# A fused attention and feed-forward kernel: the feed-forward part's preparation moved into attention's program, in smaller pieces, with the first normalisation on ScalarE

## The chip, the cores and the metric

The kernel runs on one core of a Trainium2 chip. The metric is device time of one execution in microseconds (us). TensorE (PE) multiplies matrices, VectorE (DVE), ScalarE (ACT) and GpSimd (POOL) work elementwise, SyncE (SP) issues most transfers. Each engine runs its own list of instructions in order, and waits on semaphores where it needs another's result.

## The reference

The input x has 2048 tokens of 256 values in fp32. Two layers follow each other, each wrapped as x + layernorm(f(layernorm(x))):

```python
# attention: 16 query heads and 8 key heads of 128, in pairs; causal
p = softmax(q1 k1 / sqrt(128)) - lam * softmax(q2 k2 / sqrt(128))   # two maps a head pair
o = p @ v                      # v is 256 wide
o = o * rsqrt(mean(o*o) + eps) * subln_w * (1 - LAMBDA_INIT)
out = o @ out_w.T + out_b
# feed-forward: fwht is the normalised Walsh-Hadamard transform
h = fwht(x * SU_ug) / 64
h = silu(h @ W_gate.T * (Ws_gate * 64)) * (h @ W_up.T * (Ws_up * 64))    # 1024 wide
out = (fwht(h * SU_dp) / 64) @ W_down.T * (Ws_dp * 64)
```

fwht is linear, so the kernel folds it, the signs and the scales into the weights.

## The kernel before

Every fp32 matrix product is done as three matmuls in a faster format (fp32r), since each operand is split into a high part (a copy, by ScalarE) and a low part (the difference, by VectorE or GpSimd): high x high, high x low, low x high. So each thing that TensorE reads has first passed over two other engines.

**Attention.** There are 4 groups of two query-head pairs that share keys and values. A group has 16 duos; a duo is one tile of 128 query tokens for each of its two head pairs, cut into 5 chunks of up to 512 keys (17 blocks of 128 together). Each duo has two halves, one for each softmax map (m = 0, 1). `attention_steps` writes the order of the whole of attention as one list of steps: S (scores of a chunk), T (transposes of mixed probabilities), PV (products with v), OT and OP (transpose and projection of an output), QP, K, V (projections), X (transposes of normalised x), LN and NX (statistics and normalising of x), WQ, WK, WO (splits of weights). A string for each half (`HALVES`, `HEAD`, `TURN_OF_GROUP`, `LAST_HALVES`) gives the order of its steps by letters. The engines walk through the same list, ScalarE and VectorE with lags of a step for some kinds (`SCALAR_LAGS`, `VECTOR_LAGS`). ScalarE computes exponentials (L543) and high parts (L558), VectorE row maxima (L647, L652) and low parts (L662), GpSimd mixes the two maps (L802, L805). `PAIR_ORDER` orders the tiles within a group; each output tile is added to `acc` in every group, so after the last group's visit it is final.

**Between.** A second block of the program folds weights. ScalarE and GpSimd scale raw weights (L1072, L1119), TensorE transposes them (L980, L989), both parts are split (L1028, L1045), TensorE multiplies by the Hadamard matrix of 128 (L1011, L1020), whose result is scaled and split (L1034, L1052). w_down first goes through three butterfly stages on VectorE and GpSimd (L1109, L1110). VectorE normalises the first 512 tokens in `norms` in four parts, each for 4 tiles.

**Feed-forward.** A third block runs over 4 chunks of 512 consecutive tokens. For each of 8 slices of 128 of the 1024 inner values TensorE computes gate and up (6 matmuls of 512 columns each, L1241), ScalarE Silu (L1280) and the high part of h (L1285), VectorE the product (L1330), GpSimd the low part (L1388). Then the product with folded w_down (L1256, L1258), whose rows are normalised and stored. Normalising of the next chunk is done between, in four parts of 4 tiles.

## Time and profile before

| | us |
|---|---|
| median of 3 runs | 1442.15 |
| lowest run | 1440.96 |
| profiled execution, its own time | 1443.69 |
| its span | 1441.6 |
| TensorE busy in the span | 1374.2 (95%) |
| VectorE busy | 1045.2 (73%) |
| ScalarE busy | 875.5 (61%) |
| GpSimd busy | 866.3 (60%) |

The span goes from the first to the last instruction; the execution's own time holds some 2 us around it. Busy shares are means over three unlike stages (attention, folding, feed-forward), so each stage has to be read by itself. Matmuls overlap in the records: how long TensorE takes for one is told by the distance between two starts, not by the duration of one.

### The profile page before, as it was taken

The page shows a single profiled execution, that of the slowest core. Times are in us where ns is not written, and L with a number is a line of the kernel's source. Part 1 is how long each engine was busy: PE and PEld are TensorE (multiplying, and loading weights), DVE is VectorE, ACT ScalarE, POOL GpSimd, SP SyncE. Part 2 cuts the span into 40 slices and gives each one's busy share as a digit, 9 for nine tenths or more (in the row PEclk, how much of TensorE's full clock was granted, in tenths as well). Part 3 has the DMA queues.
Part 4 walks back from the last instruction along what each step waited for, and adds up shares of the span by engine and source line. Part 5 has one row for each costly group of instructions (what it writes and reads, how often), then busy time and mean ns, then how long its engine had stood idle before and what let it go on. Part 6 is the DMA issues. An engine that isn't in the chain of part 4 may idle for free. (4 is left out here: it accounts for less than half of the span.)

```text
span 1441.6 us, 26446 instructions
## 1 busy us (share of the span) xinstructions
PE 1374.2 (95%) x8344; PEld 1214.6 (84%) x8344; DVE 1045.2 (73%) x2628; ACT 875.5 (61%) x2465; POOL 866.3 (60%) x1332
## 2 busy tenths in 40 slices
PE   5899999999999999999999999999999999569998
PEld 4789999988989999889899998898999998547887
DVE  5677778776687788766777777777778877576654
ACT  3466666666576766666666676656766667353331
POOL 7556666665666666647676656556766666335454
PEclk9999999999999999999999999999999999879999
DMA  3000000000000000000000000000000000310000
GB/s 128 1 30 1 1 1 1 1 16 1 10 22 2 1 2 1 16 1 1 31 1 1 2 1 2 16 1 1 1 1 1 1 1 1 104 43 1 11 16 33
DMA packets 14806, 18.36 MB, mean 13 GB/s; under 512 B 4432, under 2 KB 12752, under 8 KB 14288
## 3 DMA queue, kind: packets, MB, share of 16 engines
q1 hardware_dynamic: 13712, 15.35, 3.3%
q8 instruction: 71, 1.16, 0.3%
q10 hardware_dynamic: 960, 1.32, 0.3%
q14 instruction: 63, 0.52, 0.1%
HBM read 14.58 MB, written 2.10 MB: 12 GB/s over the span
## 5 line engine op out<-in xcount | busy, mean ns | idle before, releaser
L543 ACT ACTIVATE e<-score_bank,negmx 128x512 f32<-128x512 f32 (+2 forms) x640 | 394.4, 626 | 72.8 <-DVE negmx L656 71.8
L805 POOL TENSOR_TENSOR e<-e,e 128x512 f32<-128x512 f32 (+3 forms) x256 | 294.5, 1150 | 21.4
L652 DVE TENSOR_REDUCE mx<-score_bank 128x1 f32<-128x512 f32 (+1 forms) x384 | 244.6, 638 | 27.2 <-PE score_bank L448 25.8
L446 PE MATMUL score_bank<-k_hi,q_hi 128*128 128x512 f32 (+2 forms) x640 | 253.9, 397 | 8.2 <-ACT e L543 6.1
L788 POOL TENSOR_TENSOR inv_s<-s,neg_one 128x1 f32<-128x1 f32 x128 | 71.0, 555 | 314.1 <-DVE s L772 313.6
L468 PE MATMUL turn_bank<-v_hl,pT_hi 128*128 128x512 f32 x679 | 251.5, 404 | 3.8 <-DVE pT_lo L662 3.8
L448 PE MATMUL score_bank<-k_hi,q_lo 128*128 128x512 f32 (+2 forms) x640 | 231.9, 362 | 0.0
L447 PE MATMUL score_bank<-k_lo,q_hi 128*128 128x512 f32 (+2 forms) x640 | 231.3, 361 | 0.0
L470 PE MATMUL turn_bank<-v_hl,pT_lo 128*128 128x256 f32 x679 | 190.8, 281 | 0.0
L802 POOL TENSOR_SCALAR e<-e,ratio 128x512 f32<-128x512 f32 (+3 forms) x256 | 177.4, 693 | 12.4
L647 DVE CUSTOM_DVE_ANT_0 score_bank<-score_bank,mask 128x384 f32<-128x384 f32 (+3 forms) x256 | 143.3, 560 | 52.2 <-PE score_bank L448 50.8
L468 PEld LDWEIGHTS turn_bank<-v_hl,pT_hi 128*128 128x128 f32 x679 | 128.1, 189 | 30.4 <-issue 4.7
L446 PEld LDWEIGHTS score_bank<-k_hi,q_hi 128*128 128x128 f32 x640 | 121.0, 189 | 26.5 <-ACT e L543 9.3
L448 PEld LDWEIGHTS score_bank<-k_hi,q_lo 128*128 128x128 f32 x640 | 120.5, 188 | 14.1
L543 ACT ACTIVATION_READ_ACCUMULATOR e<-score_bank,negmx 128x1 f32 x640 | 131.5, 205 | 0.0
L470 PEld LDWEIGHTS turn_bank<-v_hl,pT_lo 128*128 128x128 f32 x679 | 128.8, 190 | 0.5
L447 PEld LDWEIGHTS score_bank<-k_lo,q_hi 128*128 128x128 f32 x640 | 121.8, 190 | 4.8
L468 PE MATMUL sum_bank<-v_hl,pT_hi 128*128 128x512 f32 x281 | 103.4, 401 | 1.3 <-DVE pT_lo L662 1.3
L558 ACT ACTIVATE pT_hi<-turn_bank 128x384 fp32r<-128x384 f32 (+3 forms) x140 | 75.5, 540 | 46.7 <-PE turn_bank L455 46.0
L662 DVE TENSOR_TENSOR pT_lo<-turn_bank,pT_hi 128x384 fp32r<-128x384 f32 (+3 forms) x140 | 84.3, 602 | 3.9 <-ACT pT_hi L558 3.4
L1388 POOL TENSOR_TENSOR h_lo<-h_f,h_hi 128x512 fp32r<-128x512 f32 x32 | 41.5, 1295 | 68.9 <-ACT h_hi L1285 68.9
L818 POOL TENSOR_TENSOR rms<-rms_b,half_neg 128x1 f32<-128x1 f32 x128 | 73.5, 574 | 10.7
(266 smaller groups left out, 3548.9 us busy)
## 6 DMA issues: line engine op xcount, KB each, us to landing
w_raw<-in_w_qkv_dram SPq DMA_DIRECT2D x3, 1024.0 KB, 4.8
w_raw<-in_w_o_dram SPq DMA_DIRECT2D x4, 512.0 KB, 3.3
out_dram<-d_out SPq DMA_DIRECT2D x16, 128.0 KB, 1.7
x_in<-in_hidden_dram SPq DMA_DIRECT2D x3, 512.0 KB, 9.5
x_res<-in_hidden_dram SPq DMA_DIRECT2D x1, 1536.0 KB, 13.0
w_raw<-in_w_qkv_dram ACTq DMA_DIRECT2D x2, 512.0 KB, 8.2
raw<-in_w_up_dram SPq DMA_DIRECT2D x2, 512.0 KB, 5.5
raw<-in_w_gate_dram SPq DMA_DIRECT2D x2, 512.0 KB, 7.7
```

Source lines behind the costliest of these rows:

```text
L446: pe.matmul(bank[:, 0:w], qh, kh, start=True, stop=False)
L447: pe.matmul(bank[:, 0:w], qh, kl, start=False, stop=False)
L448: pe.matmul(bank[:, 0:w], ql, kh, start=False, stop=True).then_inc(s_full, 1)
L468: pe.matmul(bank[:, :], pT_hi[:, q % PT_SLOTS, b * P:(b + 1) * P], v_hl[:, kt, :], start=(kt == 0), stop=False)
L470: mm = pe.matmul(bank[:, 0:HID], pT_lo[:, q % PT_SLOTS, b * P:(b + 1) * P], v_hl[:, kt, 0:HID], start=False, stop=(kt == i))
L543: act.activation(e, S[k % NS][:, 0:w], ACT.Exp, bias=negmx[:, d % 2, m, s:s + 1], accum_out=ssum[:, d % 4, s, m, c:c + 1]).then_inc(s_act, 1)
L558: act.activation(pT_hi[:, q % PT_SLOTS, 0:w], bank_for(kind, what)[:, 0:w], ACT.Copy).then_inc(t_hi, 1)
L647: dve.tensor_tensor_reduce(out=S[k % NS][:, 0:w], in0=S[k % NS][:, 0:w], in1=mask[:, BANK - w:], scale=1.0, scalar=LOWEST, op0=ALU.add, op ...
L652: dve.tensor_reduce(mx[:, d % 2, m, s, c:c + 1], S[k % NS][:, 0:w], X, ALU.max)\
L662: dve.tensor_tensor(pT_lo[:, q % PT_SLOTS, 0:w], bank_for(kind, what)[:, 0:w], pT_hi[:, q % PT_SLOTS, 0:w].bitcast(F32), ALU.subtract)\
L802: pool.tensor_scalar(b, b, ratio[:, d % 4, s:s + 1], 0.0, ALU.mult, ALU.add)\
L805: pool.tensor_tensor(a, a, b, ALU.add).then_inc(p_pool, 1)
```

## The change

The two later blocks of the program are gone. Their work becomes steps of the same list: HAD (the Hadamard matrix, built on GpSimd), FB (sum or difference of two halves of gate and up weights, which arrive already transposed), FH (split of that), F (fold by the matrix and split), N (one part of normalising for two tiles: parts 0 to 3 as before, each in two halves), Z (transposes of normalised tiles), G and U (gate and up of one slice, with HH for h's split), DB (pieces of w_down's butterflies), DN (product with w_down). The last group visits its tiles in another order (`LAST_ORDER`), outermost pairs first, so that a feed-forward chunk's four tiles (`chunk_tiles`) are final before attention ends. Strings for single halves of the last group (`LAST_GROUP`) say where N and Z (letter N), FH and F (f), FB (b), HAD (H) stand; in `LAST_HALVES` each U issues one gate or up block, and `with_gated` hangs further steps behind them. Tiles of attention whose last use has passed hold the new data. Scales of gate and up are applied at Silu and at the product rather than to the weights.

At the start, normalising of x (NX) goes from GpSimd to ScalarE, transfers are reordered, four of eight V units of the first group come before its first scores, and the split of w_o comes a half later.

```diff
+WS_COL = SUBLN_COL + CT
+SU_COL = WS_COL + 2 * JT
+SUD_COL = SU_COL + CT
+COLS = SUD_COL + JT
...
 PAIR_ORDER = (3, 7, 4, 2, 5, 1, 6, 0)
+LAST_ORDER = (0, 7, 1, 6, 2, 5, 3, 4)
...
-HEAD = {0: 'SKSVSVQSVS', 1: 'SVSVSQVSS', 2: 'SVSSQSVS', 3: 'TSTSSOSTPSoQTPPTP'}
+HEAD = {0: 'SKSVSQSVS', 1: 'SVSSQSVS', 2: 'SSSQSS', 3: 'TSTSSOSTPSoQTPPTP'}
...
-LAST_HALVES = ('ToTPTToOP', 'TTOTPPTPO', 'ToTTTOoPo')
+LAST_GROUP = {5: 'TSTSSOSTPSoQTPPTPH', 12: 'TSSTSSTPbTSoQTPPbPTO',
+              13: 'TSTSSNOSTPSoNQTPPTP', 14: 'TSSTSSTPNTSoQTPPNPTO', 15: 'TSTSSNOSTPSfoNQTPPTP',
+              16: 'TSSTSSTPNTSfoQTPPNPTO', 17: 'TSTSSNOSTPSfoQNTPPTP', 18: 'TSSTSSTPbTSfoQTPPbPTO',
+              20: 'TSSTSSTPTSfoQTPPPTO', 21: 'TSTSSNOSTPSfoNQTPPTP', 22: 'TSSTSSTPNTSfoQTPPNPTO',
+              23: 'TSTSSNOSTPSfoNQTPPTP', 24: 'TSSTSSTPNbTSoQTPPNbPTO', 25: 'TSTSSNOSTPSoQNTPPTP',
+              26: 'TSSTSSTPTSfoQTPPPTO', 27: 'TSTSSOSTPSfoQTPPTP', 28: 'TSSTSSfTPbTSfoQTPPbPTO',
+              30: 'TSSTSSfTPTSfoQTPPPTO', 31: 'TSTSSfOSTPSfoQTPPTP'}
+LAST_HALVES = ('ToTPTToOPUU', 'UTUTOTPUPTPO', 'TUoTUTTOUoPUo')
...
+def chunk_tiles(c):
+    return (2 * c, 2 * c + 1, TILES - 2 - 2 * c, TILES - 1 - 2 * c)
+def pair_of(u):
+    return (LAST_ORDER if u // (DUOS // 2) == GROUPS - 1 else PAIR_ORDER)[u % (DUOS // 2)]
...
-    for kind, what in (("LN", 0), ("WK", 0), ("NX", 0), ("LN", 1), ("WQ", 0), ("X", 0), ("X", 1), ("NX", 1),
-                       ("K", (0, 0, 0)), ("LN", 2), ("X", 2), ("X", 3), ("K", (0, 1, 0)), ("NX", 2), ("QP", (0, 1, 0)),
-                       ("K", (0, 0, 1)), ("QP", (0, 1, 1)), ("LN", 3), ("X", 4), ("X", 5), ("K", (0, 1, 1)), ("NX", 3),
-                       ("QP", (0, 0, 0)), ("K", (0, 0, 2)), ("LAM", None), ("QP", (0, 0, 1)), ("X", 6), ("X", 7),
-                       ("K", (0, 1, 2)), ("K", (0, 0, 3))):
+    for kind, what in (("LN", 0), ("LN", 1), ("NX", 0), ("WK", 0), ("NX", 1), ("X", 0), ("X", 1), ("WQ", 0), ("LN", 2),
+                       ("X", 2), ("X", 3), ("NX", 2), ("K", (0, 0, 0)), ("K", (0, 1, 0)), ("X", 4), ("X", 5), ("LN", 3),
+                       ("V", (0, 0)), ("V", (0, 1)), ("QP", (0, 1, 0)), ("QP", (0, 1, 1)), ("K", (0, 0, 1)), ("NX", 3),
+                       ("K", (0, 1, 1)), ("V", (0, 2)), ("V", (0, 3)), ("LAM", None), ("QP", (0, 0, 0)),
+                       ("QP", (0, 0, 1)), ("K", (0, 0, 2)), ("X", 6), ("X", 7), ("K", (0, 1, 2)), ("K", (0, 0, 3))):
...
+    norms = [x for c in range(2) for x in norm_steps(c, range(4)) + turn_steps(c)]
+    folds = [x for n in range(0, 8, 2) for x in fold_steps(n)]
+    hadamard = [("HAD", None)]
+    added_up = [("FB", n) for n in range(8)]
+    gated = [0]
+    with_gated = {
+        2: norm_steps(2, (0,)), 4: norm_steps(2, (1,)) + [("DB", 0), ("DB", 1)], 5: [("DB", 2), ("DB", 3)],
+        6: norm_steps(2, (2,)) + [("DB", 4), ("DB", 5)], 7: [("DB", 6), ("DB", 7)], 8: norm_steps(2, (3,)),
+        9: [("DB", i) for i in range(8, 12)], 10: [("DB", i) for i in range(12, 16)], 11: [("FH", 8), ("FH", 9)],
+        12: [("F", 8), ("F", 9), ("FH", 10), ("FH", 11)], 13: [("F", 10), ("F", 11)], 14: turn_steps(2),
+        16: norm_steps(3, (0,)), 18: norm_steps(3, (1,)), 20: norm_steps(3, (2,)), 22: norm_steps(3, (3,))}
+    def emit_gated():
+        k, up = divmod(gated[0], 2)
+        gated[0] += 1
+        emit("U" if up else "G", k)
+        if not up and k > 0:
+            emit("HH", k - 1)
+        if up:
+            for what in with_gated.get(k, ()):
+                emit(*what)
...
-    while exps_due or factors_due or mixes_due:
-        emit("END", None)
-    for what in to_turn:
-        emit("OT", what)
-    for what in to_project:
-        emit("OP", what)
+    assert not (exps_due or factors_due or mixes_due or norms or folds or added_up)
+    while to_turn or to_project:
+        if to_turn:
+            emit("OT", to_turn.pop(0))
+        emit_gated()
+        if to_project:
+            emit("OP", to_project.pop(0))
+    for c in range(FFN_CHUNKS):
+        while gated[0] < 2 * JT * (c + 1):
+            emit_gated()
+        if c + 1 == FFN_CHUNKS:
+            emit("HH", JT * FFN_CHUNKS - 1)
+        if c > 0:
+            for n in range(QB * (c - 1), QB * c):
+                emit("DN", n)
+                if n == QB:
+                    for what in turn_steps(3):
+                        emit(*what)
+    for n in range(QB * (FFN_CHUNKS - 1), QB * FFN_CHUNKS):
+        emit("DN", n)
+    emit("DEND", None)
...
+            def wug(f, co):
+                return ((k_hi[:, co, 3 * BANK:], k_lo[:, co, 3 * BANK:]),
+                        (v_hl[:, 12 + co, :], v_hl[:, 14 + co, :]),
+                        (wq_hi[:, co, :], wq_lo[:, co, :]),
+                        (v_hl[:, 10 + co, :], w3_lo[:, co, :]))[f]
+            wd_hl = v_hl[:, 0:JT, :]
+            wd_a, wd_b = e1[:, 0:4, :], e1[:, 5:9, :]
+            wsd_row = out_b_row
+            z = bv
+            gate = w_raw[:, 1, :].rearrange("p (a n) -> p a n", a=2)
+            h_f = v_sum
...
+                sp.wait_ge(kv_dve, last_value_split + 1)
+                load_input(0)
+                sp.wait_ge(t_full, t_use["Z", (0, 1)] + 1)
+                load_input(1)
+                sp.wait_ge(folded_ready, 2)
+                sp.dma_start(raw_w(2), w_ug[2]).then_inc(raw_landed[2], 16)
+                sp.wait_ge(folded_ready, 4)
+                sp.dma_start(raw_w(3), w_ug[3]).then_inc(raw_landed[3], 16)
+                sp.wait_ge(t_full, t_use["Z", (1, 1)] + 1)
+                load_input(2)
+                sp.wait_ge(t_full, last_turn[CHUNKS * (ALL_DUOS - 1) - 1] + 1)
+                sp.dma_start(wd_a, w_d.rearrange("p (q n) -> p q n", q=4)).then_inc(wd_landed, 16)
...
+                    elif kind in ("G", "U"):
+                        c, jt = divmod(what, JT)
+                        up = kind == "U"
+                        b = 2 * (what % 2) + up
+                        if what < 2:
+                            pe.wait_ge(s_act, last_score - (last_score - b) % NS + 1)
+                        else:
+                            pe.wait_ge(h_ready if up else g_act, what - 1)
+                        if jt == 0 and not up:
+                            pe.wait_ge(t_lo, t_use["Z", (c, 1)] + 1)
+                        if c == 0 and jt % 2 == 0 and not up:
+                            pe.wait_ge(t_lo, t_use["F", jt + 1] + 1)
+                        at, n = 2 * (jt % 2) * P + up * P, 0
+                        for ct in range(CT):
+                            w_hi_part, w_lo_part = wug(jt // 2, ct)
+                            for w, x in ((w_hi_part, xT_hi), (w_hi_part, xT_lo), (w_lo_part, xT_hi)):
+                                mm = pe.matmul(S[b][:, :], w[:, at:at + P], x[:, ct, Z_COLS[c]:Z_COLS[c] + BANK],
+                                               start=(n == 0), stop=(n == 5))
+                                n += 1
+                        mm.then_inc(u_full if up else g_full, 1)
...
+                    elif kind == "NX":
+                        act.wait_ge(rstd_ready, what + 1)
+                        for t in range(4 * what, 4 * what + 4):
+                            act.activation(x_in[:, t, :], x_in[:, t, :], ACT.Identity, bias=shift[:, t:t + 1],
+                                           scale=rstd[:, t:t + 1]).then_inc(xn_ready, 1)
...
+                    elif kind == "N":
+                        c, part, half = what
+                        base = 24 * c + 8 * part + 4 * half
+                        pair = [(x, chunk_tiles(c)[x]) for x in (2 * half, 2 * half + 1)]
+                        if part == 0:
+                            dve.wait_ge(r_free, max(r_use["OP", last_visit[t]] for _, t in pair) + 1)
+                        if part in (0, 2):
+                            dve.wait_ge(n_step, base)
+                            for x, t in pair:
+                                dve.bn_stats(n_stats[:, x, :], acc[:, t, :]).then_inc(n_step, 1)
+                            dve.wait_ge(n_step, base + 2)
+                            for x, t in pair:
+                                dve.bn_aggr(n_mv[:, x, :], n_stats[:, x, :]).then_inc(n_step, 1)
+                        elif part == 1:
+                            dve.wait_ge(y_rstd, c + 1)
+                            dve.wait_ge(xr_landed, 32 * c + 32)
+                            for x, t in pair:
+                                dve.scalar_tensor_tensor(out=acc[:, t, :], in0=acc[:, t, :], scalar=n_rs[:, x:x + 1],
+                                                         in1=z[:, x, :], op0=ALU.mult, op1=ALU.add)\
+                                   .then_inc(n_step, 1)
+                            dve.wait_ge(n_step, base + 2)
+                            for x, t in pair:
+                                dve.tensor_scalar(acc[:, t, :], acc[:, t, :], n_mr[:, x:x + 1], None, ALU.subtract)\
+                                   .then_inc(n_step, 1)
+                        else:
+                            dve.wait_ge(z_rstd, c + 1)
+                            for x, t in pair:
+                                dve.tensor_scalar(z[:, x, :], acc[:, t, :], n_mv[:, x, 0:1], n_rs[:, x:x + 1],
+                                                  ALU.subtract, ALU.mult).then_inc(z_ready, 1)
...
+                    elif kind == "U":
+                        b, at = 2 * (what % 2) + 1, WS_COL + 2 * (what % JT) + 1
+                        dve.wait_ge(g_act, what + 1)
+                        dve.wait_ge(u_full, what + 1)
+                        if what == 0:
+                            dve.wait_ge(wt_lo_ready, 8)
+                        if what >= 2:
+                            dve.wait_ge(h_lo_ready, what - 1)
+                        dve.scalar_tensor_tensor(out=h_f[:, what % 2, :], in0=S[b][:, :], scalar=col[:, at:at + 1],
+                                                 in1=gate[:, what % 2, :], op0=ALU.mult, op1=ALU.mult)\
+                           .then_inc(h_ready, 1)
...
+                    elif kind == "FB":
+                        f, co = divmod(what, CT)
+                        pool.wait_ge(raw_landed[f], 16)
+                        if what == 0:
+                            pool.wait_ge(had_ready, 1)
+                        if what >= 2:
+                            pool.wait_ge(wt_lo_ready, what - 1)
+                        pool.tensor_tensor(folded[:, co, :], raw_w(f)[:, 0, :], raw_w(f)[:, 1, :],
+                                           ALU.subtract if co else ALU.add).then_inc(folded_ready, 1)
...
+                    elif kind == "DB" and what < 8:
+                        if what < 4:
+                            pool.wait_ge(wd_landed, 16)
+                            pool.wait_ge(wsd_landed, 16)
+                            unit = wd_a[:, what, :].rearrange("p (a n) -> p a n", a=2)
+                            scales = wsd_row[:, :].rearrange("p (a n) -> p a n", a=1).broadcast_to([P, 2, HID])
+                            pool.tensor_tensor(unit, unit, scales, ALU.mult).then_inc(wd_pool, 1)
+                        else:
+                            pool.wait_ge(wd_pool, 2 if what < 6 else 4)
+                            pool.wait_ge(t_full, last_turn[CHUNKS * ALL_DUOS - 1] + 1)
+                            units, op = slice(what // 6 * 2, what // 6 * 2 + 2), what % 2
+                            pool.tensor_tensor(wd_b[:, units, op * HID:(op + 1) * HID], wd_a[:, units, 0:HID],
+                                               wd_a[:, units, HID:2 * HID], ALU.subtract if op else ALU.add)\
+                                .then_inc(wd_pool, 1)
...
-        with ExitStack() as ffn:
...
```

**VectorE, half 14 of the last group.** Before, around the mixing of that duo's fourth chunk (e is a chunk of exponentials, pT_lo the low part of transposed probabilities):

```order
L662 TENSOR_TENSOR pT_lo<-proj_bank,pT_hi 128x384
L780 SCALAR_TENSOR_TENSOR e_64<-e_65,ratio,e_64 128x512
L652 TENSOR_REDUCE mx<-score_bank 128x1
L662 TENSOR_TENSOR pT_lo<-sum_bank,pT_hi 128x384
L647 ISA score_bank,mx<-score_bank,mask 128x384
L647 ISA mx 128x1
L656 TENSOR_REDUCE negmx<-mx 128x1
```

And in the changed kernel:

```order
L1234 SCALAR_TENSOR_TENSOR e_64<-e_65,ratio,e_64 128x384
L1023 TENSOR_TENSOR pT_lo<-sum_bank,pT_hi 128x384
L1174 SCALAR_TENSOR_TENSOR acc<-acc,n_rs,bv 128x256 x2
L1179 TENSOR_SCALAR acc<-acc,n_mr 128x256 x2
L1008 ISA score_bank,mx<-score_bank,mask 128x384
L1008 ISA mx 128x1
L1017 TENSOR_REDUCE negmx<-mx 128x1
```

Between a split of probabilities and the masked maximum of the next scores now stand four instructions that normalise two tiles.

**TensorE, the end of attention.** Before, behind the last output projection:

```order
L512 MATMUL turn_bank<-wo_lo,oT_hi 128x256
L512 MATMUL turn_bank<-wo_hi,oT_lo 128x256
L245 UNCONDITIONAL_BRANCH
L969 UNCONDITIONAL_BRANCH
L980 MATMUL turn_bank<-ident,raw 128x128 x8
L980 MATMUL sum_bank<-ident,raw 128x128 x4
```

In the changed kernel, the first gate block (S banks from xT and folded weights, which lie in k_hi and k_lo):

```order
L689 MATMUL turn_bank<-v_hl,pT_lo 128x256
L782 MATMUL score_bank<-xT_hi,k_hi 128x512
L782 MATMUL score_bank<-xT_lo,k_hi 128x512
L782 MATMUL score_bank<-xT_hi,k_lo 128x512
```

The transposes of raw weights are gone, and gate and up stand between products of attention's last duo.

**ScalarE, the start.** Before:

```order
L617 ACTIVATE wkv_hi<-w_raw 128x1024
L610 ACTIVATE wq_hi<-w_raw 128x1024
L604 ACTIVATE xT_hi<-score_bank 128x512 x2
L593 ACTIVATE k_hi<-turn_bank,col 128x512
L604 ACTIVATE xT_hi<-score_bank 128x512 x2
```

Changed:

```order
L872 ACTIVATE x_in<-x_in,shift,rstd 128x256 x4
L890 ACTIVATE wkv_hi<-w_raw 128x1024
L872 ACTIVATE x_in<-x_in,shift,rstd 128x256 x4
L877 ACTIVATE xT_hi<-score_bank 128x512
L883 ACTIVATE wq_hi<-w_raw 128x1024
L877 ACTIVATE xT_hi<-score_bank 128x512 x2
```

The copy of the first transposes now follows two rounds of normalising.

## Rows read from the trace of the kernel before

**Rows 1.** The page: the granted clock in 40 slices, in tenths.

```profile
PEclk9999999999999999999999999999999999879999
```

**Rows 2.** Busy time by stretch; columns: us, then each engine's busy us (instructions), clock, DMA.

```profile
600.00:610.00 10.00, 9.04 (x53) 7.43 (x52) 8.87 (x23) 6.99 (x20) 5.08 (x11) 1.00 0.15 54
1108.00:1118.00 10.00, 10.00 (x66) 8.84 (x64) 9.15 (x22) 6.76 (x21) 4.96 (x7) 1.00 0.00 1
1005.00:1215.00 210.00, 209.95 (x1330) 189.20 (x1329) 163.19 (x417) 142.73 (x430) 137.79 (x222) 1.00 0.00 1
0.00:50.00 50.00, 31.44 (x161) 26.30 (x162) 27.52 (x73) 18.31 (x31) 28.11 (x35) 0.97 0.28 93
...
1250.00:1300.00 50.00, 30.87 (x117) 23.66 (x118) 36.59 (x80) 23.62 (x43) 14.16 (x16) 0.69 0.32 105
1300.00:1350.00 50.00, 48.25 (x221) 38.62 (x220) 30.95 (x74) 19.83 (x36) 26.74 (x29) 1.00 0.00 1
```

**Rows 3.** TensorE's timeline; columns: start, duration, line, operation, tiles, shapes, idle before and releaser.

```profile
17.89 0.63 PE L481 MATMUL turn_bank<-xT_hi,wkv_lo 128*128 128x512 f32 x1
18.32 0.63 PE L481 MATMUL turn_bank<-xT_hi,wkv_hi 128*128 128x512 f32 x1
...
904.43 0.47 PE L468 MATMUL turn_bank<-v_hl,pT_hi 128*128 128x512 f32 x1 [0.96 <-DVE pT_lo L662]
...
911.49 0.39 PE L446 MATMUL score_bank<-k_hi,q_hi 128*128 128x512 f32 x1
911.72 0.40 PE L447 MATMUL score_bank<-k_lo,q_hi 128*128 128x512 f32 x1
```

**Rows 4.** TensorE's timeline at the end of attention and of folding.

```profile
1225.67 0.50 PE L468 MATMUL turn_bank<-v_hl,pT_hi 128*128 128x512 f32 x1 [1.11 <-DVE pT_lo L662]
...
1244.66 0.36 PE L512 MATMUL turn_bank<-wo_hi,oT_hi 128*128 128x256 f32 x1 [1.00 <-DVE oT_lo L678]
...
1245.33 0.28 PE L512 MATMUL turn_bank<-wo_hi,oT_lo 128*128 128x256 f32 x1
...
1292.30 0.79 PE L1241 MATMUL score_bank<-xT_hi,wug_hi 128*128 128x512 f32 x1 [1.41 <-DVE xT_lo L1305]
```

**Rows 5.** The timeline of the start.

```profile
7.75 5.56 POOL L854 TENSOR_SCALAR x_in<-x_in,mv,rstd 128x256 f32<-128x256 f32 x4
...
13.46 1.94 PE L429 MATMUL score_bank<-ident,x_in 128*128 128x128 f32 x8 [13.46 <-POOL x_in L854]
...
16.90 0.77 PE L481 MATMUL turn_bank<-xT_hi,wkv_hi 128*128 128x512 f32 x1 [1.51 <-DVE xT_lo L727]
...
72.17 0.50 PE L446 MATMUL score_bank<-k_hi,q_hi 128*128 128x512 f32 x1 [3.89 <-ACT e L543]
...
73.53 0.69 PE L446 MATMUL score_bank<-k_hi,q_hi 128*128 128x384 f32 x1 [0.32 <-ACT e L543]
```

**Rows 6.** Groups by line and shape; columns: count, busy us, mean ns, idle before.

```profile
L1388 POOL TENSOR_TENSOR h_lo<-h_f,h_hi 128x512 fp32r<-128x512 f32 x32 | 41.5, 1295 | 68.9 <-ACT h_hi L1285 68.9
...
L1052 DVE SCALAR_TENSOR_TENSOR wug_lo<-score_bank,su_col,wug_hi 128x512 fp32r<-128x512 f32 x8 | 5.8, 746 | 1.7 <-ACT wug_hi L1034 1.7
...
L1072 ACT ACTIVATE raw<-raw,scaled_col 128x256 f32<-128x256 f32 x8 | 3.6, 499 | 11.8 <-DMA raw<-in_w_up_dram 11.8
```

**Rows 7.** DMA issues of the page; last columns: KB, us to landing.

```profile
raw_d<-in_w_down_dram SPq DMA_DIRECT2D x1, 1024.0 KB, 9.8
```

**Rows 8.** VectorE's timeline while it normalises four tiles.

```profile
1257.24 1.38 DVE L897 TENSOR_SCALAR acc<-acc,y_mr 128x256 f32<-128x256 f32 x4
...
1298.50 1.39 DVE L886 BATCH_NORM_STATS2 y_stats<-acc 128x6 f32<-128x256 f32 x4
1299.93 0.38 DVE L889 BATCH_NORM_AGGREGATE y_mv<-y_stats 128x2 f32<-128x6 f32 x4
1304.40 2.00 DVE L893 SCALAR_TENSOR_TENSOR acc<-acc,y_rs,x_res 128x256 f32<-128x256 f32 x4
1306.43 2.13 DVE L897 TENSOR_SCALAR acc<-acc,y_mr 128x256 f32<-128x256 f32 x4
```

889 lines of the change are left out of this document (363 added, 526 removed).

## The prediction

> **What bounds the kernel now.** I read the page first. TensorE's clock is at full speed in nearly every slice [rows 1], and in an ordinary stretch of 210 us of attention TensorE is busy for 209.95 us, VectorE for 163.2 (78%), ScalarE for 142.7, GpSimd for 137.8 [rows 2]. So attention is bound by TensorE, and only two things shorten the time: less work on TensorE, or fewer holes in it. The timeline says what full pace is: a matmul of 512 columns starts 0.23 us after the one before it, and at the lower of the clock's two levels (1.2 against 2.4 GHz) 0.43 us [rows 3].
>
> Then I looked for the holes. The large one lies between attention and the feed-forward part: the last output projection starts at 1245.33, the first gate matmul at 1292.30 [rows 4]. In the 50 us around it TensorE is busy for 30.9 at a granted clock of 0.69, while VectorE is busy for 36.6: folding weights and normalising is a chain over the other engines [rows 2]. Just ahead of it attention runs dry: five waits of 0.6 to 1.3 us from 1225.67 to 1244.66, 5.0 us together [rows 4]. The third place is the start: first transposes at 13.46, first projection at 16.90, and a wait of 3.89 us at 72 [rows 5]; TensorE is busy for 31.4 of the first 50 us [rows 2].
>
> **The large hole.** The change puts folding, the weights' splits, and the normalising of chunks 0 and 1 into halves 12 to 31 of the last head group; the first gate matmul then follows the last ordinary product steps on TensorE directly. What goes is 1292.30 less 1245.45 (the last projection's start plus 0.12), 46.9 us. What of it must still be done on TensorE moves: 24 fold matmuls at 0.23, 5.6 us (40 before; the transposes of raw weights are gone, and the gate/up fold's 128-step now adds or subtracts halves of the weights on GpSimd), and the 8 transposes of z for chunk 0, 0.9 us (eight took 1.94 at the lower level [rows 5]). Net **-40.4**. Nothing hides these 6.5 us: TensorE is the bound there.
>
> **The dry end of attention.** The last three halves now carry gate and up matmuls between transposes and products, 10 blocks of six (1.4 us each). Each of the five waits is shorter than one such block. But the table load for Silu (once, as before) and the gate's activation now stand ahead of probability copies on ScalarE. I take **-3.5** of the 5.0; ends 0 and -5. In the later feed-forward part the 50 us from 1300 have 1.75 us of idle TensorE [rows 2], spent on the next chunk's transposes that are now early: **-1.5**.
>
> **GpSimd while w_down is folded.** It had all of w_down's butterfly halves inside the hole. Now pairs 4 to 7 of gate and up give GpSimd, beside h_lo at 1.30 us [rows 6], two additions or products each of the same shape: 3.9 us against TensorE's 2.8 for twelve matmuls, 4.4 us too much over four pairs, with roughly one pair of slack since h_f waits for the h_lo of two pairs ago. Queued behind them on GpSimd is the next h_lo; VectorE's h_f waits for that, TensorE's next bank for h_f. **+2.5**; ends 0 and +9.8, the latter if w_down itself (1 MB, 9.8 us before [rows 7]) has not landed: its load waits on SyncE for the transposes of the last duo but one, some 15 us ahead of its first use.
>
> **VectorE in the last group: what I fear most.** Two halves issue 30 score matmuls, 17 transposes and 34 products, and 28 matmuls for output and queries: 109. The 210 us hold 1330 [rows 2], so two halves take 17.2 us, one half 8.6. Added to VectorE per chunk of four tiles: statistics twice (1.39 and 0.38 each time), scale and add 2.00, subtract 2.13, final scale 2.1: 9.8 us [rows 8]. Chunk 0's lie in halves 13 to 16 with two splits of folded weights (0.75 each, as the folded row [rows 6]), chunk 1's in 21 to 24 with three. Four halves on TensorE: 34.4 us, 35 with what is added. On VectorE: 0.78 x 34.4 = 26.7, plus 9.8 plus 1.5 (or 2.25): 38.0 and 38.7. VectorE becomes the bound of eight halves. If it could be busy all the time, that costs 3.0 + 3.7 = 6.7 us. The busiest stretch in which TensorE lost nothing has VectorE at 9.15 of 10 us; another at 8.87 lost 0.96 us of TensorE [rows 2]. At 92% it costs 6.3 + 7.1 = 13.4. I take **+10**, between them. The ends are +3 (the other engines run ahead and absorb it) and +34: all that is added, 2 x 9.8 + 16 x 0.75 + 4 transposed halves of z at 0.7, exposed. ScalarE gets 20 copies of 0.6 in 175 us and stays under 80%; GpSimd gets eight additions of 1.3 and four sets of 1.3: under 80% too. Both I cost at nothing beyond this.
>
> Here the durations themselves depend on the neighbour: the same four subtractions took 1.38 us at 1257 in the hole, and 2.13 at 1306 beside GpSimd's h_lo [rows 8]. I used the slow values, since GpSimd is busy for 66% of attention [rows 2]. GPSIMD Engine Reference of the Trainium skill (Specifications) says why that may be: GpSimd shares its SBUF interfaces with VectorE, with contention when VectorE runs in a two-port mode or reads two SBUF inputs. The splits of folded weights now read two SBUF tiles, where they read a PSUM bank; by that rule they would cost more than 0.75, and GpSimd's mixing would slow down too. That speaks against the change; no row of this case prices it for the split.
>
> **The start.** Normalising moves from GpSimd (5.56 us for four tiles [rows 5]) to ScalarE, at about 0.5 a tile (scaling raw weights of the same shape took 0.50 [rows 6]), 2 us for four; statistics of tiles 4 to 7 come before weights. x is thus ready at about 10 instead of 13.3. But on ScalarE the copy of the first transposes now stands behind the second normalisation and a weight copy of 1.1, so the first projection starts near 16.5, hardly earlier than 16.90. The gain comes after: K and V units follow back to back, four V units (12 matmuls of 256 columns, at half of 0.23 each, 1.4 us) are done before the first scores, in time that was waiting; I count 5 us by 40 us. Four V units less in the first halves should also take most of the 3.89 us at 72, where v_sum waited behind GpSimd's mixing, while the split of w_o a half later takes some back: 2.5. **-7.5**; ends 0 and -14.
>
> **Sum**, against the profiled execution's own 1443.7 (1.5 above the runs' median): 1443.7 - 40.4 - 3.5 - 1.5 + 2.5 + 10 - 7.5 = 1403.3. Against the median: **1402**, 2.8% less.
>
> **Rivals.**
> *Absorbed.* VectorE's surplus disappears in slack (+3), the start gives 11: 1402 - 7 - 3.5 = 1391. For it: single waits of TensorE in attention are short and rare, so there is slack of unknown depth. Against it: the surplus is a sum over four halves, longer than any buffer of two or three tiles. Chance 0.22.
> *VectorE exposed.* An in-order VectorE puts a pair of normalised tiles (2.1 us) ahead of the probability split that TensorE's products wait for, every time: +34 in place of +10: 1426. For it: the only waits in attention name exactly that split (0.96 at 904 [rows 3]). Against it: other steps fill the time between transpose and product. Chance 0.13.
> *The clock falls: slower than before.* After the 3.89 us wait at 72, a matmul of 384 columns took 0.69 us [rows 5], where 512 take 0.39 at the full level, so TensorE had fallen to the lower one; after the 0.96 at 904 it had not (0.47 for 512) [rows 3]. If VectorE's lumps make longer waits, each is followed by work at 0.43 for 0.23, 1.85 times as long. Forecast and before are 40 us apart: that is eaten once 47 us of full-pace work in halves 13 to 31 and the drain run at the lower level. At half of their 175 us it costs 75: 1477. Against it: the lumps are 2.1 us at most. TensorE: Matmul & The Clock Gate (HAM oscillation) describes this pattern, a TensorE throttled anew after each wait between short bursts of work; in this trace the low clock stands only beside long holes. Chance 0.04.
> *The start does not gain* (ScalarE takes over GpSimd's role as the late one): 1410, within the forecast's range.
>
> **How the numbers follow.** Forecast with its own range of 1392 to 1414: 0.60; absorbed 0.22; exposed 0.13; clock 0.04; the rest unforeseen. A measurement tells 2% from no change: 1413.3 and 1471. Faster: nearly all of the forecast, all of absorbed, a little of exposed: 0.82. Same: 0.14. Slower: 0.04. The range that holds 8 in 10 goes from 1385 (start at its end, surplus absorbed) to 1419 (half-way into the exposed case).
>
> **What would show it.** In the profile after: no stretch with TensorE under 80% between 1200 and the end; VectorE above 90% in two stretches some 35 us long, about 165 and 90 us before attention's last products, with TensorE waiting for pT_lo there; GpSimd above 90% just after them; first projection at 16 to 17; granted clock near 1.00 from 80 us on. Wrong would be: waits of TensorE over 3 us in the last group, or a new hole at the first gate matmul.

## The result and the profile after

| | before | changed |
|---|---|---|
| median of the runs, us | 1442.15 | 1420.67 |
| profiled execution, its own time | 1443.69 | 1416.04 |
| its span | 1441.6 | 1414.2 |

One more execution of the kernel before took 2739.1 us and is left out of its median. The ratio of the runs is 0.984, with an interval of [0.983, 0.986]: 1.6% faster, so within the 2% called no change. The prediction said 1402, 2.8% less, with a range up to 1419. A second timing of the same kernel gave 1419.08, ratio 0.983 [0.982, 0.985]. The medians fell by 21.5 us, and by 24.0 in the second timing (1443.06 before), the spans of the two profiled executions by 27.4: the traces show some 3 to 6 us more than the runs do.

The page first, its line of TensorE and the granted clock in 40 slices:

```profile
PE 1357.1 (96%) x8280; PEld 1200.0 (85%) x8280; DVE 1052.5 (74%) x2612; ACT 877.6 (62%) x2471; POOL 858.8 (61%) x1342
...
PEclk9999999999999999999999999999999999999999
```

The slices of 8 and 7 tenths of [rows 1] are gone. Busy time by stretch, as in [rows 2] (busy us of PE, PEld, DVE, ACT, POOL, then clock, DMA share and GB/s):

```profile
0.00:50.00 50.00, 32.52 (x178) 27.51 (x179) 28.05 (x75) 25.36 (x48) 13.05 (x30) 1.00 0.28 93
...
1050.00:1100.00 50.00, 48.00 (x300) 42.47 (x299) 44.48 (x118) 31.99 (x96) 35.56 (x56) 1.00 0.00 1
1100.00:1150.00 50.00, 48.45 (x311) 43.47 (x310) 43.07 (x111) 35.77 (x102) 34.42 (x54) 1.00 0.10 33
1150.00:1200.00 50.00, 45.74 (x285) 40.14 (x284) 44.19 (x111) 32.33 (x93) 33.59 (x52) 1.00 0.04 12
1200.00:1250.00 50.00, 47.42 (x288) 41.92 (x287) 37.82 (x94) 34.21 (x96) 36.62 (x56) 1.00 0.06 22
1250.00:1300.00 50.00, 45.59 (x224) 36.54 (x223) 34.45 (x60) 18.91 (x39) 30.14 (x33) 1.00 0.00 0
1300.00:1350.00 50.00, 47.34 (x216) 38.38 (x216) 36.47 (x75) 22.34 (x42) 22.79 (x29) 0.97 0.06 19
```

The 30.87 us of TensorE in 50 from 1250 [rows 2] are 45.59 now. But 1050 to 1200, which was ordinary attention (209.95 of 210), now has 1.6 to 4.3 us of idle TensorE in every 50, with VectorE at 86 to 89%. Over stretches of 35 us, the length that the prediction named, VectorE reaches 97% and 91% (same columns):

```profile
1074.00:1109.00 35.00, 31.95 (x198) 27.55 (x196) 33.90 (x83) 21.30 (x65) 22.74 (x37) 1.00 0.00 1
1150.00:1185.00 35.00, 30.88 (x192) 27.05 (x191) 31.88 (x82) 21.03 (x61) 22.71 (x35) 1.00 0.01 1
```

The first 50 us hardly changed (31.44 before). TensorE's timeline, places that answer to [rows 4, 5]:

```profile
10.39 1.94 PE L648 MATMUL score_bank<-ident,x_in 128*128 128x128 f32 x8 [10.39 <-ACT x_in L872]
16.73 0.77 PE L700 MATMUL turn_bank<-xT_hi,wkv_hi 128*128 128x512 f32 x1 [1.56 <-DVE xT_lo L1088]
64.41 0.50 PE L665 MATMUL score_bank<-k_hi,q_hi 128*128 128x512 f32 x1 [2.99 <-ACT e L811]
84.06 0.47 PE L687 MATMUL turn_bank<-v_hl,pT_hi 128*128 128x512 f32 x1 [2.28 <-DVE pT_lo L1023]
1082.71 0.63 PE L674 MATMUL turn_bank<-ident,e 128*128 128x128 f32 x4 [1.71 <-DVE oT_lo L1039]
1159.01 0.39 PE L733 MATMUL turn_bank<-wo_hi,oT_hi 128*128 128x256 f32 x1 [2.62 <-DVE v_hl L1139]
1246.57 0.40 PE L782 MATMUL score_bank<-xT_hi,k_hi 128*128 128x512 f32 x1
1294.93 0.50 PE L782 MATMUL score_bank<-xT_hi,v_hl 128*128 128x512 f32 x1 [1.10 <-DVE v_sum L1203]
1299.71 0.50 PE L782 MATMUL score_bank<-xT_hi,wq_hi 128*128 128x512 f32 x1 [1.70 <-DVE v_sum L1203]
1304.04 0.57 PE L756 MATMUL turn_bank<-wkv_hi,had 128*128 128x512 f32 x1 [2.66 <-DVE wkv_lo L1131]
```

The first gate matmul starts at 1246.57 without a wait: the large hole is closed. Behind the first transposes every wait of 0.9 us or more names VectorE or ScalarE, and the longest is just under 3 us; one of 0.70 at 1012.24 names GpSimd.

**Where the time is.** In each trace I gave every matmul its full-pace time (distance of two starts: 0.232 us for 512 columns, 0.174 for 384, 0.1175 for 256, 0.0875 for a transpose and 0.09 once behind transposes). What the start of the next matmul is late by is lost: waiting or a low clock. Each sum is good to about 1 us, by the choice of these times.

| TensorE, us | before | changed | difference | predicted |
|---|---|---|---|---|
| lost, 0 to 100 | 35.5 | 34.4 | -1.1 | -7.5 |
| lost, 100 to 975 | 7.9 | 6.7 | -1.2 | 0 |
| lost, last group (to 1225; to 1246) | 1.6 | 16.8 | +15.2 | +10 |
| lost, attention's end and hole to 1292; end and w_down, 1246 to 1325 | 36.7 | 10.5 | -26.2 | -33.4 |
| lost, the rest | 6.7 | 0.6 | -6.1 | -1.5 |
| full-pace work | 1346.7 | 1338.7 | -8.0 | -8.0 |

The differences add up to -27.4, the difference of the two spans. The predictions add up to -40.4, as their sum did; the hole's -40.4 is split here into its idle time (with -3.5 and +2.5 beside it) and the work that went.

The last two rows of lost time do not hold the same work. In the changed kernel 1246 to 1325 already has 192 of the 384 gate and up matmuls, which before stood behind 1292. Up to its 192nd, at 1355.5, the kernel before lost some 5.9 of the 6.7 us. Like for like, the end, the hole and the first half of the feed-forward part went from about 42.6 to 10.6 us, 32 less where 34.9 were predicted, and the second half hardly changed.

### The profile page after: what moved, and what is told of

Read it like the earlier page. It is cut to its first block and busy times, and to the rows that moved or that the text cites. A ratio compares the mean times of both kernels' runs of the same rounds, so it can differ in the third digit from the quotient of the medians.

```text
span 1414.2 us, 26342 instructions
## 1 busy us (share of the span) xinstructions
PE 1357.1 (96%) x8280; PEld 1200.0 (85%) x8280; DVE 1052.5 (74%) x2612; ACT 877.6 (62%) x2471; POOL 858.8 (61%) x1342
## 5 line engine op out<-in xcount | busy, mean ns | idle before, releaser
L687 PE MATMUL turn_bank<-v_hl,pT_hi 128*128 128x512 f32 x590 | 217.4, 402 | 4.6 <-DVE pT_lo L1023 4.6
L689 PE MATMUL turn_bank<-v_hl,pT_lo 128*128 128x256 f32 x590 | 165.3, 280 | 0.0
L687 PEld LDWEIGHTS turn_bank<-v_hl,pT_hi 128*128 128x128 f32 x590 | 110.9, 188 | 27.4 <-issue 5.8
L689 PEld LDWEIGHTS turn_bank<-v_hl,pT_lo 128*128 128x128 f32 x590 | 111.4, 189 | 0.7
L687 PE MATMUL sum_bank<-v_hl,pT_hi 128*128 128x512 f32 x290 | 107.2, 403 | 2.3 <-DVE pT_lo L1023 2.2
L826 ACT ACTIVATE pT_hi<-turn_bank 128x384 fp32r<-128x384 f32 (+3 forms) x150 | 80.2, 536 | 41.6 <-PE turn_bank L674 39.8
L1023 DVE TENSOR_TENSOR pT_lo<-turn_bank,pT_hi 128x384 fp32r<-128x384 f32 (+3 forms) x150 | 89.8, 599 | 2.9 <-ACT pT_hi L826 2.4
L674 PE MATMUL turn_bank<-ident,e 128*128 128x128 f32 x508 | 79.9, 272 | 1.9 <-DVE oT_lo L1039 1.9
L689 PE MATMUL sum_bank<-v_hl,pT_lo 128*128 128x256 f32 x290 | 81.3, 280 | 0.0
```

The lines of the kernel that those rows point to most:

```text
L687: pe.matmul(bank[:, :], pT_hi[:, q % PT_SLOTS, b * P:(b + 1) * P], v_hl[:, kt, :], start=(kt == 0), stop=False)
L689: mm = pe.matmul(bank[:, 0:HID], pT_lo[:, q % PT_SLOTS, b * P:(b + 1) * P], v_hl[:, kt, 0:HID], start=False, stop=(kt == i))
L826: act.activation(pT_hi[:, q % PT_SLOTS, 0:w], bank_for(kind, what)[:, 0:w], ACT.Copy).then_inc(t_hi, 1)
L1023: dve.tensor_tensor(pT_lo[:, q % PT_SLOTS, 0:w], bank_for(kind, what)[:, 0:w], pT_hi[:, q % PT_SLOTS, 0:w].bitcast(F32), ALU.subtract)\
```

## The experiments

A run's median is in us; its ratio to runs of the kernel before on the same chip has an interval of about 0.0015 to either side, some 2 us, so where a difference is smaller the traces decide. The runs were made on four chips, on which the kernel before has medians of 1441.29 to 1443.06; a median from another chip than the second timing's can be off against it by up to 1.8 us, and the ratio is the fairer measure. Against the ratio of the second timing (0.9832) scalar_norm is 4.2 us faster, narrow_norms 4.8, narrow_norms_splits 10.2, narrow_butterflies 5.5, spread 1.7, folds_moved 1.4, best 7.8, and nx_on_gpsimd 2.0 slower, each to some 3 us. "Lost" is counted as above, in the three places in question, for the profiled execution (the wait before the first matmul is in the first).

| kernel | median | ratio | 0 to 100 | last group | 1246 to 1325 |
|---|---|---|---|---|---|
| changed, second timing | 1419.08 | 0.9832 | 36.4 | 17.4 | 10.7 |
| old_start | 1419.69 | 0.9842 | 35.5 | 17.6 | 11.0 |
| nx_on_gpsimd | 1419.13 | 0.9846 | 36.6 | 17.0 | 10.7 |
| v_in_halves | 1418.17 | 0.9827 | 35.8 | 17.5 | 10.8 |
| wo_early | 1419.47 | 0.9838 | 35.0 | 18.7 | 10.9 |
| narrow_norms | 1414.05 | 0.9799 | 36.0 | 12.7 | 10.4 |
| narrow_norms_splits | 1407.63 | 0.9761 | 34.7 | 8.3 | 9.6 |
| narrow_butterflies | 1412.82 | 0.9794 | 34.4 | 19.1 | 4.0 |
| scalar_norm | 1413.67 | 0.9803 | 36.4 | 12.2 | 8.6 |
| spread | 1416.11 | 0.9820 | 35.2 | 17.1 | 9.5 |
| folds_moved | 1415.61 | 0.9822 | 36.5 | 15.7 | 9.4 |
| best | 1409.18 | 0.9778 | 35.1 | 13.9 | 4.9 |
| best_wo_early | 1410.37 | 0.9770 | 35.0 | 12.9 | 5.8 |

### The kernel again, and its start

> The changed kernel once more, with nothing different in it. Its profiled execution before was 1416.0 us, 4.6 below the median of its other runs (1420.7) at a granted clock of 0.996 against 0.994. If that is how the clock happens to fall in single executions, this kernel's median is again 1420 to 1421 and its profile's own time 1416 to 1422; if the median comes out at 1416, the earlier timing was the odd one, and the prediction's range would nearly have held it.

It measured 1419.08; its profiled execution took 1419.2. The first profiled execution was the odd one: its granted clock in 0 to 50, 50 to 100 and 1150 to 1200 was 1.00, 0.97 and 1.00, this one's is 0.97, 0.93 and 0.97. The waits over 0.9 us behind 100 us recur to 0.1 us, with one more of 0.92 at 604; at 72 us 1.62 became 0.91. So one execution of this kernel is good to 3 us, and the spans compared in the result section sit about 3 us low for the changed kernel.

> The changed kernel with the whole start of before: normalising of x on GpSimd, the old order of the first steps and of their transfers, all eight V units of the first group in its halves, split of w_o a half earlier. The prediction gave the new start 7.5 us. Theory 1 (from the two traces, TensorE's idle and slow time in the first 100 us being 35.5 us before and 34.4 after): the new start gains 1.1 us, so this kernel takes 1421.8 us, 1420 to 1424. Theory 2: the start gained its 7.5 and the records hide it (slow single executions): 1428. Theory 3: the new start costs, its gain having gone to waits at 64 and 84 us: under 1419.

Edit: the old list of first steps, `HEAD`, transfers and place of w_o's split, and

```diff
-                            act.activation(x_in[:, t, :], x_in[:, t, :], ACT.Identity, bias=shift[:, t:t + 1],
-                                           scale=rstd[:, t:t + 1]).then_inc(xn_ready, 1)
+                            pool.tensor_scalar(x_in[:, t, :], ...)
```

1419.69, just under the range of theory 1, which is the nearest. The new start is worth 0.6 us by the medians and nothing that the intervals can tell.

> The changed kernel with one part undone: the first normalising of x is on GpSimd again (four tiles took 5.56 us there), the new order of the start's steps and transfers stays. The whole start undone cost 0.6 us. Theory 1 (x ready 3 us earlier is worth little, since the copies on ScalarE behind it are what is late): 0 to 2 us slower than the changed kernel, 1419 to 1421. Theory 2 (ScalarE's part gains 3 to 5 and the new order, with four V units ahead of the first scores, loses as much): 1422 to 1424.

Edit: the last two lines alone. 1419.13, though TensorE's first projection is 5 us later than in the changed kernel; by the ratio, 0.9846, it is 2.0 us slower, within the noise and within theory 1. From its trace, the places that answer to 16.73, 64.41 and 84.06 in the changed kernel:

```profile
21.72 0.78 PE L700 MATMUL turn_bank<-xT_hi,wkv_hi 128*128 128x512 f32 x1
66.53 0.50 PE L665 MATMUL score_bank<-k_hi,q_hi 128*128 128x512 f32 x1 [3.02 <-ACT e L811]
85.11 0.47 PE L687 MATMUL turn_bank<-v_hl,pT_hi 128*128 128x512 f32 x1 [2.27 <-DVE pT_lo L1018]
```

A delay of 4.99 at the first projection is 2.12 at the score matmul at 66 and 1.05 at the product at 85. So most of a late x is gone by 85 us: these 85 us are mainly set by something else.

> The changed kernel with one part of the new start undone: all eight V units of the first group are again in its first halves, none ahead of the first scores. The prediction gave those four units and the back-to-back projections 5 us by 40 us, and 2.5 more at 72. The whole start undone cost 0.6 us, the first normalising put back on GpSimd nothing, though its first projection came 5.0 us later (21.72 against 16.73). Theory 1 (the first 85 us are set by the turn-taking of scores, maxima and exponentials, which wait in order behind V's copies wherever these stand): within 1.5 us of the changed kernel, 1418 to 1420.5. Theory 2 (V ahead of the scores costs what the earlier x gains): 1414 to 1416. Theory 3 (V ahead gains the predicted 5 to 7, and the rest of the new order loses it): 1424 or more.

```diff
-HEAD = {0: 'SKSVSQSVS', 1: 'SVSSQSVS', 2: 'SSSQSS', 3: 'TSTSSOSTPSoQTPPTP'}
+HEAD = {0: 'SKSVSVQSVS', 1: 'SVSVSQVSS', 2: 'SVSSQSVS', 3: 'TSTSSOSTPSoQTPPTP'}
```

(and the four V steps out of the first list)

```profile
16.63 0.77 PE L700 MATMUL turn_bank<-xT_hi,wkv_hi 128*128 128x512 f32 x1 [1.55 <-DVE xT_lo L1088]
32.63 0.47 PE L700 MATMUL turn_bank<-xT_hi,wkv_hi 128*128 128x512 f32 x1 [2.76 <-DVE k_lo L1053]
71.36 0.63 PE L665 MATMUL score_bank<-k_hi,q_hi 128*128 128x512 f32 x1 [4.39 <-ACT e L811]
83.95 0.47 PE L687 MATMUL turn_bank<-v_hl,pT_hi 128*128 128x512 f32 x1 [1.79 <-DVE pT_lo L1023]
```

1418.17, theory 1 again. With V units ahead of the scores the wait of 4.39 at 71 is 1.62, but 2.99 stand at 64, and at 84 both are at the same place within 0.11 us. What makes the one at 64 is seen in the changed kernel's VectorE and ScalarE:

```profile
62.27 0.76 DVE L1064 TENSOR_TENSOR v_sum<-turn_bank,bv 128x256 f32<-128x256 f32 x2
63.06 0.63 ACT L866 ACTIVATE v_hl<-v_sum 128x512 fp32r<-128x512 f32 x1 [2.48 <-DVE v_sum L1064]
63.59 0.67 ACT L811 ACTIVATE e<-score_bank,negmx 128x512 f32<-128x512 f32 x1
```

ScalarE waits 2.48 us in order for a V sum that VectorE does behind two maxima; the exponential behind it frees the bank that TensorE waits for.

> The changed kernel with the split of w_o a half earlier, as before the change. TensorE waits 2.28 us for pT_lo at 84.06 there, while ScalarE and VectorE split w_o (1.72 and some 2.2 us from 79.5). Theory 1 (that wait goes, and nothing comes in its place): 2 us less, 1417 to 1418. Theory 2 (a wait of about the same size opens a half earlier, as the 3.89 us at 72 in the kernel before): 1419 to 1421.

```diff
-        if h == 3:
+        if h == 2:
             for s in range(2):
                 emit("WO", (0, s))
```

1419.47, theory 2: the wait of 2.28 at 84 goes, and smaller ones of 0.39 and 1.05 come at 72.6 and 74.4, where ScalarE copies w_o between exponentials (0.90 for two at 71.06). The trace has 1.4 us less lost by 100, which the timing does not show.

### The last group

> The kernel before with one part of the change alone: the last head group visits its pairs of tiles outermost first (0, 7, 1, 6, 2, 5, 3, 4 in place of 3, 7, 4, 2, 5, 1, 6, 0). The prediction gave this nothing. Theory 1 (from the trace after: waits of 1.02, 0.47 and 0.70 us on pT_lo, acc and e between 980 and 1012, at the turn into the last group, which narrowing the normalising left as they were): 2 to 4 us slower than before. Theory 2 (those waits belong to what else was put into the last group): within 1 us of before.

```diff
-        e = 2 * PAIR_ORDER[d % DUOS // 2] + d % 2
+        e = 2 * pair_of(d // 2) + d % 2
```

1443.1 against 1442.09, ratio 1.0008 [0.9998, 1.0018]: about 1 us slower, and the interval goes from nothing to 2.6. Theory 1, 2 to 4 us, is not borne out, except at its lowest end. The wait of 1.02 on pT_lo is there at 981.55 with this edit alone, so the order does cause it; but less than 1 us more than before is lost in 975 to 1000, and the wait for GpSimd's mixing at 1012 (0.70) is not there. In the changed kernel the 16 small instructions of HAD stand ahead of that mixing on GpSimd for 5.4 us from 1004.71; that they make the wait was not tested by a run.

> The changed kernel with VectorE's normalising instructions of chunks 0 and 1 cut to 8 of 256 columns; the other columns are left out. Every instruction, wait and semaphore stays. Full width these are 9.8 us a chunk at the durations before, some 16 us in all beyond what an instruction of 8 columns costs. Theory 1 (VectorE is the bound of eight halves in the last group): the 15 us that TensorE loses between 975 and 1250 fall to 5 to 7, the kernel takes 1411 us, 1408 to 1413. Theory 2 (the waits come from the order of tiles, from the folded weights' splits, or from chains that end at VectorE but are not its load): 1417 or more. Theory 3 (exposed one by one): the whole 16 us come back, 1405.

```diff
-                                dve.tensor_scalar(acc[:, t, :], acc[:, t, :], n_mr[:, x:x + 1], None, ALU.subtract)\
+                                dve.tensor_scalar(acc[:, t, 0:n_w], acc[:, t, 0:n_w], n_mr[:, x:x + 1], None, ALU.subtract)\
```

(`n_w` is 8 for chunks 0 and 1; the same in the other normalising lines.) 1414.05, 5.0 us off, between theories 1 and 2. The last group loses 12.7 in place of 17.4: normalising is a cause, and not the only one.

> The changed kernel with VectorE's normalising of chunks 0 and 1 cut to 8 of 256 columns, as in narrow_norms (1414.0 against 1419.1), and with it the low parts of six of eight added-up and of six of eight folded gate and up weights cut to 8 of 512 columns; the other columns are left out. Theory 1 (VectorE's sum of work is the bound, and these splits are 12 x some 0.8 = 9 us of it): 3 to 5 us less than narrow_norms, 1409 to 1411; the waits of 1.07, 1.64 and 0.40 us at 1156, 1176 and 1210 in that trace go. Theory 2 (what is left of the waits comes from the order of tiles and from chains, not from load): within 1.5 us of narrow_norms, 1412.5 to 1415.

```diff
-                        dve.tensor_tensor(wt_lo[:, what % 2, :], source, wt_hi[:, what % 2, :].bitcast(F32),
+                        dve.tensor_tensor(wt_lo[:, what % 2, 0:s_w], source[:, 0:s_w],
+                                          wt_hi[:, what % 2, 0:s_w].bitcast(F32),
```

1407.63, another 6.4 off by medians and some 5.5 by ratios, nearest to theory 1 and beyond its range. The waits at 1156 and 1176 go, as it said; one of 0.99 on oT_lo at 1100 stays. Its stretches:

```profile
1050.00:1100.00 50.00, 49.19 (x312) 44.06 (x310) 43.43 (x124) 33.70 (x103) 37.03 (x57) 1.00 0.01 1
1100.00:1150.00 50.00, 49.47 (x315) 44.76 (x316) 40.18 (x112) 35.84 (x103) 34.32 (x57) 1.00 0.10 33
1150.00:1200.00 50.00, 49.63 (x316) 44.49 (x316) 41.93 (x122) 35.71 (x104) 33.95 (x53) 1.00 0.04 12
```

TensorE is busy for 148.3 of 150 us, against 142.2 in the changed kernel. VectorE is still busy for 87% there in the first 50. The stretches of 35 us from above, first of this run, then of best, which comes further down and leaves nothing out:

```profile
1074.00:1109.00 35.00, 33.66 (x213) 29.59 (x212) 32.93 (x91) 23.86 (x72) 24.89 (x40) 1.00 0.00 1
1150.00:1185.00 35.00, 34.63 (x220) 30.76 (x220) 30.11 (x90) 24.04 (x70) 26.05 (x42) 1.00 0.05 16
```

```profile
1150.00:1185.00 35.00, 32.72 (x199) 28.91 (x198) 28.87 (x76) 24.22 (x71) 24.58 (x39) 0.95 0.00 1
```

In 1150 to 1185 VectorE at 86% costs TensorE less than 1 us of lost time in the narrowed kernel, and at 82% about 4 in best, where 91% cost 4.7 in the changed kernel. In 1074 to 1109 VectorE at 94% costs 2, where 97% cost 4.3 in the changed kernel. So the loss does not follow a busy share alone, 92% or another; what stands in a row counts too. In the changed kernel, VectorE ahead of the wait at 1159.01:

```profile
1154.81 1.36 DVE L1174 SCALAR_TENSOR_TENSOR acc<-acc,n_rs,bv 128x256 f32<-128x256 f32 x2
1156.21 1.23 DVE L1179 TENSOR_SCALAR acc<-acc,n_mr 128x256 f32<-128x256 f32 x2
1157.36 0.69 DVE L1008 CUSTOM_DVE_ANT_0 score_bank<-score_bank,mask 128x512 f32<-128x512 f32 x1
1157.97 0.13 DVE L1008 DVE_READ_ACCUMULATOR2_ANT mx<- 128x1 f32 x1
1158.14 0.16 DVE L1017 TENSOR_REDUCE negmx<-mx 128x1 f32<-128x3 f32 x1
1158.21 0.74 DVE L1139 SCALAR_TENSOR_TENSOR v_hl<-turn_bank,su_s,v_hl 128x512 fp32r<-128x512 f32 x1
```

The fold's result holds a turn bank from 1154.36 (ScalarE's copy) until VectorE has subtracted it at 1158.95. Two normalised tiles (2.6 us) and a masked maximum stand ahead, and TensorE's next output projection wants that bank. The same four instructions take 1.5 us from 1273.15, beside single columns on GpSimd: about 1.1 of the 2.6 us is VectorE waiting for GpSimd, as the last section shows.

> The changed kernel with two of VectorE's normalising steps on ScalarE in all four chunks: the subtraction, and the final subtract and scale, as one activation each with scale and bias; GpSimd negates the means. VectorE loses 4.2 of 9.8 us a chunk, ScalarE gains 8 activations of about 0.5. Theory 1 (VectorE's load is the bound where chunks 0 and 1 are normalised, 5.0 us came back when its five instructions a tile were cut to 8 columns): half of that and a little in the later chunks: 1415.5 to 1417. Theory 2 (ScalarE becomes the late one, its exponentials stand behind activations that wait for VectorE): 1419 or more.

```diff
-                                dve.tensor_scalar(acc[:, t, :], acc[:, t, :], n_mr[:, x:x + 1], None, ALU.subtract)\
-                                   .then_inc(n_step, 1)
+                                act.activation(acc[:, t, :], acc[:, t, :], ACT.Identity, bias=n_mr[:, x:x + 1])\
+                                   .then_inc(n_sub, 1)
```

(and the final scale in the same way, two steps behind) 1413.67, 5.4 off by medians, 4.2 by ratios, more than theory 1 asked: last group 12.2 lost, and 2.1 less behind it. That is as much as narrow_norms gave, as far as the runs can tell, without leaving anything out.

> The changed kernel with the same steps, and VectorE's splits of folded weights moved out of the halves that normalise: the first added-up weights and their splits to halves 8 to 11 of the last group, the first folds at 17 and 18, the second four steps at 19 and 20 in place of 20 to 23. Nothing is left out. Cutting those splits to 8 columns took 6.4 us off. Theory 1 (it is the coincidence with normalising in the same halves; elsewhere VectorE has room): 3 to 5 us less than the changed kernel's 1419.1, 1414 to 1416. Theory 2 (VectorE has no room anywhere in the last group, only the place of the wait changes): 1418 to 1420.

```diff
-              16: 'TSSTSSTPNTSfoQTPPNPTO', 17: 'TSTSSNOSTPSfoQNTPPTP', 18: 'TSSTSSTPbTSfoQTPPbPTO',
-              20: 'TSSTSSTPTSfoQTPPPTO', 21: 'TSTSSNOSTPSfoNQTPPTP', 22: 'TSSTSSTPNTSfoQTPPNPTO',
+              16: 'TSSTSSTPNTSoQTPPNPTO', 17: 'TSTSSNOSTPSfoQNTPPTP', 18: 'TSSTSSTPTSfoQTPPPTO',
+              19: 'TSTSSfOSTPSfoQTPPTP', 20: 'TSSTSSfTPTSfoQTPPPTO', 21: 'TSTSSNOSTPSoNQTPPTP',
```

The median fits theory 1, but the ratio, 0.9822 [0.9806, 0.9838], overlaps that of the changed kernel, which it beats by 1.4 us, and the last group loses only 1.7 us less. Inconclusive as to size; less than the 6.4 that it was to explain.

### w_down's butterflies

> The changed kernel with the eight last butterfly pieces of w_down on VectorE cut to 8 of 512 columns; the rest is left out. They took 8.9 us of VectorE in gate/up pairs 9 and 10 (4.19 for four, 2.97 for three, 1.77 for one), and the prediction counted only GpSimd's part of w_down. Theory 1 (these, unpriced, make the waits of 1.10, 1.70 and 2.66 us on VectorE at 1295 to 1304, and the granted clock of 0.97 behind them): 4 to 6 us less, 1415 to 1417. Theory 2 (the waits there belong to GpSimd's low parts and additions, as the prediction priced them at 2.5): at most 1.5 us less, 1419 or more.

```diff
-                        dve.tensor_tensor(to[:, first + step * op, :], source[:, first, :], source[:, first + step, :],
+                        dve.tensor_tensor(to[:, first + step * op, 0:8], source[:, first, 0:8], source[:, first + step, 0:8],
```

1412.82, 6.3 off by medians, 5.5 by ratios, and 4.0 lost from 1246 to 1325 in place of 10.7: theory 1, in its place, with somewhat more than it asked. Of TensorE's waits of 1.10, 1.70 and 2.66 there, one of 0.78 is left. All eight of these instructions, by line (duration in ns: least, median, most), in the changed kernel, then narrowed:

```profile
L1193 DVE TENSOR_TENSOR e<-e x8: 679/894/1776, 1292.4 to 1300.8; 128x512 f32<-128x512 f32 x8
```

```profile
L1193 DVE TENSOR_TENSOR e<-e x8: 152/160/1251, 1295.4 to 1299.6; 128x8 f32<-128x8 f32 x8
```

> The changed kernel with VectorE's eight last butterfly pieces of w_down two a pair in pairs 9 to 12, in place of four a pair in 9 and 10, and the splits and folds of w_down one pair later. Nothing is left out. Cutting them to 8 columns gave 6.3 us. Theory 1 (it is the lump that hurts: four pieces of 1.0 us with h_f behind them, against 2.8 us of TensorE a pair): 3 to 6 us less than the changed kernel, 1413 to 1416. Theory 2 (it is VectorE's sum over these pairs): nothing comes back, 1418 to 1420.

```diff
-        9: [("DB", i) for i in range(8, 12)], 10: [("DB", i) for i in range(12, 16)], 11: [("FH", 8), ("FH", 9)],
+        9: [("DB", 8), ("DB", 9)], 10: [("DB", 10), ("DB", 11)], 11: [("DB", 12), ("DB", 13)],
+        12: [("DB", 14), ("DB", 15), ("FH", 8), ("FH", 9)], 13: [("F", 8), ("F", 9), ("FH", 10), ("FH", 11)],
```

1416.11: 3.0 off by medians, 1.7 by ratios, and 1.2 less lost from 1246 to 1325: between the theories. The wait of 1.70 became 0.31, but that on wkv_lo grew from 2.66 to 3.03, since the fold stands right behind its split; in best, with the fold a pair later, it is 0.15.

> Three things together: scalar_norm (5.4 us under the changed kernel), folds_moved, and w_down's last butterfly pieces two a pair in pairs 8 to 11 instead of four a pair in 9 and 10 (two a pair in 9 to 12 gave 3.0, with a wait of 3.03 us left where the fold came right behind its split; here the fold comes a pair later). Theory 1 (the three work on different waits): 5.4 + 5 for the butterflies + 2 to 4 for the folds less what scalar_norm already gave there: 1406 to 1409. Theory 2 (they share one cause, VectorE's load, and the first edit has taken most of it): 1410 to 1412.

1409.18, ratio 0.9778 [0.9763, 0.9792]: 2.2% under the kernel before, and at the upper end of theory 1. From 1246 to 1325 it loses 4.9 us, nearly as little as with the butterflies cut (4.0); TensorE's waits there:

```profile
1293.25 0.50 PE L787 MATMUL score_bank<-xT_hi,v_hl 128*128 128x512 f32 x1 [1.85 <-DVE v_sum L1215]
1296.62 0.50 PE L787 MATMUL score_bank<-xT_hi,wq_hi 128*128 128x512 f32 x1 [0.30 <-DVE v_sum L1215]
1301.24 0.50 PE L761 MATMUL sum_bank<-wkv_hi,had 128*128 128x512 f32 x1 [0.15 <-DVE wkv_lo L1150]
```

In the last group moved folds added nothing to scalar_norm: 13.9 against 12.2, with a wait of 2.12 on oT_lo at 1158.29.

> The best version so far (1409.2) with the split of w_o a half earlier. By theory 1 for wo_early 1407 to 1408, by theory 2 1409 to 1410.5.

1410.37, ratio 0.9770 [0.9756, 0.9785]. Not told apart from best.

## Why the prediction was wrong

The spans fell by 13.0 us less than predicted. Two steps failed and make about that much by themselves: the gain of the start, and VectorE's pieces of w_down's butterflies, for which the sum has no term. The last group lost some 5 us more than its term, outside the halves for which the term was worked out, and a larger gain in the feed-forward part made part of it good.

**The hole: right.** First gate matmul without a wait, full-pace work 8.0 us less, idle time of the hole gone (some 32 us lost there before, none now). Its -40.4 stood.

**The start: wrong, -7.5 predicted, about -1 found.** The step that failed is "K and V units follow back to back, four V units [...] are done before the first scores, in time that was waiting; I count 5 us by 40 us", with 2.5 more for the wait at 72. It priced a delay at one place as if it ran on to the end. nx_on_gpsimd shows that it doesn't: 5 us late at 17 us are 1 us at 85 us. The first 85 us are a pipeline being filled, in which scores, maxima, exponentials and V's sums take turns on in-order engines; v_in_halves shows the same time lost whether V is done early or late, only in another wait. That this holds for all orders of these steps is not shown; three were tried.

**VectorE in the last group: about right where it was counted, +10 predicted; +15.2 found in the whole group** (17.4 in the second trace). Both stretches with VectorE above 90% are there, at 97% and 91% of 35 us, and from 1050 to 1200 TensorE loses some 10 us, where the kernel before lost nothing. What comes on top stands elsewhere: about 2.5 us from 975 to 1050, the turn of the group (about 1 by last_order) and the wait on GpSimd at 1012; and about 3 from 1200 on, of which 1.7 are the first wait of attention's end. That the size came out is in part luck. The sum priced VectorE's busy time against TensorE's; narrow_norms_splits and best show that the loss does not follow that share alone. The wait that was named was the wrong one, too: from 1050 to 1200 TensorE waits 4.0 us for oT_lo, 2.6 for the split of a fold (v_hl) and only 0.5 for pT_lo. Of the 17.4 us narrow_norms_splits recovers 9.1; the rest no run took apart.

**GpSimd while w_down is folded: the wrong engine.** "+2.5; ends 0 and +9.8" counted additions and products on GpSimd. The stretch from 1250 has POOL at 30.14 of 50 us, not above 90%, and w_down landed in 4.9 us. The eight later butterfly pieces, which the diff gives to VectorE in pairs 9 and 10, were in no term of the sum. They cost 5.5 to 6.3 us, by the run that cuts them. This omission alone takes 1402 to 1408. Beside that the 2.5 cannot be seen by itself: with the pieces narrowed 4.0 us are lost from 1246 to 1325, and no wait of TensorE there names GpSimd.

**The dry end and the later part.** Of five waits of 5.0 us, three are left (1.47 at 1242.74, 0.67, 0.93), 3.1 us: -1.9 for the -3.5. The later feed-forward part gave 6.1 where 1.5 were predicted. Before, 5.9 of its 6.7 us stood ahead of its 192nd gate and up matmul, 2.8 of them before 1300 and 3.1 from 1300 to 1350. The price was taken from the 1.75 us of idle time in the second of these stretches; it left out the first, and late matmuls behind a wait, which do not show in a busy share.

**Sum.** Against -40.4: start +6.4, attention's middle -1.2, last group +5.2, the end and w_down +7.2, later part -4.6 (+2.6 for these two together, whose border lies in different work): +13.0, and -27.4 is what the spans show. The median of all executions lies 3 to 5 us above the profiled one, which takes it out of the range. The result lies between the forecast and the rival in which VectorE's lumps are exposed (1426), but it did not come about in that rival's way: most of the miss stands outside the last group, and the probability split that the rival names is hardly waited for. The clock rival did not come: 1.00 or 0.97 in every 50 us from 1050 on. "The start does not gain" came true.

## What to carry to other kernels

A gain at the start of a pipeline was worth here only what was left of it where the pipeline is full: follow one late instruction through to there, or delay it in a run. Work that is moved under a bound engine is paid by the row of instructions ahead of a bank's release on an in-order engine as well as by that engine's busy share, so look for both, the share over the length of the stretch in question and not over a round 50 us. Put pieces of about a microsecond apart, and give each engine's list of a moved step its own term in the sum, all of them.

## What the runs showed of the hardware

Some of VectorE's instructions do not get slower beside GpSimd by a factor: they wait for it. In the changed kernel, VectorE and GpSimd at one place:

```profile
1274.05 0.62 DVE L1179 TENSOR_SCALAR acc<-acc,n_mr 128x256 f32<-128x256 f32 x2
...
1277.81 2.57 DVE L1179 TENSOR_SCALAR acc<-acc,n_mr 128x256 f32<-128x256 f32 x2
...
1278.89 2.64 POOL L1347 TENSOR_TENSOR e<-e,out_b_row 128x512 f32<-128x512 f32 x2
...
1285.93 2.58 POOL L1352 TENSOR_TENSOR e<-e 128x512 f32<-128x512 f32 x2
1286.00 2.66 DVE L1184 TENSOR_SCALAR bv<-acc,n_mv,n_rs 128x256 f32<-128x256 f32 x2 [0.80 <-POOL n_rs L1339]
```

Two subtractions take 0.62 us when GpSimd works on single columns, and 2.57 beside its products of 512 columns at 1.3 us each: one of VectorE's for one of GpSimd's. With the work taken away the wait stays, in the kernel with narrow butterflies:

```profile
1295.31 2.56 POOL L1359 TENSOR_TENSOR q_lo<-v_sum,q_hi 128x512 fp32r<-128x512 f32 x2
```

```profile
1295.41 1.25 DVE L1193 TENSOR_TENSOR e<-e 128x8 f32<-128x8 f32 x1
1296.78 0.75 DVE L1203 SCALAR_TENSOR_TENSOR v_sum<-score_bank,col,w_raw 128x512 f32<-128x512 f32 x1
1297.44 0.88 DVE L1193 TENSOR_TENSOR e<-e 128x8 f32<-128x8 f32 x4
```

Eight columns took 1.25 us while GpSimd was in an instruction of 1.34. Of the four at 1297.44 the first took 0.45, since GpSimd's second instruction ran until 1297.87, and the others 0.15 to 0.17. Each held instruction of VectorE in this section ends 0.02 to 0.17 us after one of GpSimd's. The one at 1296.78, which reads a PSUM bank and one SBUF tile, was not held (0.75), nor were the changed kernel's 32 statistics of 256 columns with their one SBUF input (0.40 to 0.42). The page SBUF — State Buffer of the Trainium skill (Who interferes with whom) says that VectorE with two SBUF inputs (beside a GpSimd instruction that reads SBUF), or in a two-port mode (which tensor_scalar can take), shares a pair of ports with GpSimd, locked for a whole instruction, and that the later one blocks. These rows agree. The prediction had quoted a milder form of this and drawn no price from it. The kernel before shows it already, in the subtractions of [rows 8] (duration in ns: least, median, most):

```profile
L897 DVE TENSOR_SCALAR acc<-acc,y_mr x16: 333/343/1365, 1257.2 to 1368.6; 128x256 f32<-128x256 f32 x16
```

The 2.13 us of the four at 1306.43, which the prediction took for a slow value of all four, are one of 1.34, beside GpSimd's h_lo, and three of 0.34. It may be part of why scalar_norm gave as much as narrow_norms: cutting columns leaves the waiting for GpSimd in place (one pair of 8 columns took 1.76 us there), moving the instruction to ScalarE takes it away too. No run separates the two.
